# Expert MLP kernel: the last three tiles reordered, with seven up products between the halves of tile 14's main product and six more ahead of tile 15's

## What is computed

```
x = x + ffn0(cond0(x))      # cond0: mix of the 64 channels by a kernel made from cond; ffn0: 8 experts, top 2, 1024x1024 each
x = x + ffn1(cond1(x))      # cond1: grouped 1D convolution, 9 taps, plus a context term
                            # ffn1: main = c1 @ weight.T
                            #       gates = gw2(relu(layernorm(c1 @ gw1.T))), top 2, softmax, capacity over all tokens
                            #       lora = sum over experts of (c1 @ lora_A[e]) * w[e] @ lora_B[e] / 16
                            #       out = main + lora
```

## Time and profile before

| | us |
|---|---|
| median of 3 runs | 852.18 |
| lowest, highest | 850.26, 853.11 |
| the profiled execution | 853.87 |
| its span in the trace | 852.0 |
| TensorE busy in the span | 816.2 |
| VectorE busy in the span | 399.9 |

### The profile page before, as it was taken

The page is one execution under the profiler, slowest core; times in us unless marked ns, Lnnn a source line. Parts: engine busy times, 40 slices in busy tenths (PEclk is TensorE's granted clock), DMA queues, the critical chain, the costliest instruction groups (busy, mean ns, idle before and its releaser), DMA issues.

```text
span 852.0 us, 13067 instructions
## 1 busy us (share of the span) xinstructions
PE 816.2 (96%) x4260; PEld 674.0 (79%) x4261; DVE 399.9 (47%) x920; ACT 216.5 (25%) x335; POOL 90.4 (11%) x137
## 2 busy tenths in 40 slices
PE   6999599999999999999999999999999999999985
PEld 5555488888888888888888888888898898889863
DVE  1388650241514215142151151486566566656597
ACT  2344241342514325242252242300100010000100
POOL 1000121011110111011110012121112111100000
PEclk9999699999999999999999999999999999999998
DMA  8888479373555525555255254675545644520048
GB/s 284 347 323 311 176 278 418 114 256 127 185 183 181 201 86 184 184 169 213 86 174 192 90 197 132 214 204 140 126 98 139 147 108 107 155 58 25 1 137 258
DMA packets 61652, 149.26 MB, mean 175 GB/s; under 512 B 6928, under 2 KB 23584, under 8 KB 60704
## 3 DMA queue, kind: packets, MB, share of 16 engines
q1 hardware_dynamic: 40960, 93.41, 33.4%
q0 software_dynamic: 9968, 36.19, 14.6%
q10 hardware_dynamic: 10704, 19.41, 6.0%
HBM read 100.74 MB, written 39.85 MB: 165 GB/s over the span
## 4 chain that ended last, share of the span: by engine, by line
PE 81%; DMA 6%; DVE 6%; issue 3%; ACT 2%; SPq 1%; ACTq 1%; DVEq 0%; POOL 0%; POOLq 0%
PE bank L1283 58%; PE bank L1322 6%; PE bank L1181 4%; PE bank L1331 4%; PE bank L1274 3%; DMA work<-in_expert_w 3%; PE bank L1385 1%; DVE work L1116 1%; PE bank L1158 1%; DVE weights L937 1%; PE bank L1229 1%; PE bank L1204 1%; PE bank L1144 1%; DMA work<-y_scratch,pos_c 1%; DMA x1p<-res 1%
## 5 line engine op out<-in xcount | busy, mean ns | idle before, releaser
L1283 PE MATMUL bank<-weights,l_hi 128*128 128x512 f32 x1696 | 523.8, 390 | 0.0
L1283 PEld LDWEIGHTS bank<-weights,l_hi 128*128 128x128 f32 x1696 | 319.4, 188 | 64.6
L1283 PE MATMUL bank<-weights,l_lo 128*128 128x512 f32 x848 | 336.0, 396 | 2.5 <-DVE l_lo L905 2.4
L1283 PEld LDWEIGHTS bank<-weights,l_lo 128*128 128x128 f32 x848 | 159.7, 188 | 35.5 <-issue 4.5
L905 DVE TENSOR_TENSOR l_lo<-bank,l_hi 128x512 fp32r<-128x512 f32 x37 | 25.6, 692 | 184.0 <-ACT l_hi L684 184.0
L937 DVE TENSOR_TENSOR weights<-work,weights 128x1024 fp32r<-128x1024 f32 x64 | 76.2, 1223 | 55.1 <-ACT weights L695 54.8
L695 ACT ACTIVATE weights<-work 128x1024 fp32r<-128x1024 f32 x64 | 65.1, 1054 | 45.9 <-DMA work<-in_expert_w 27.6
L540 POOL DMA_INDIRECT work<-c_scratch,idx x37 | 42.4, 1146 | 196.2 <-PE bank L1274 195.9
L1322 PE MATMUL bank<-conv_sb,x1p 128*128 128x128 f32 x512 | 59.8, 275 | 1.1 <-DMA x1p<-res 1.1
L1322 PEld LDWEIGHTS bank<-conv_sb,x1p 128*128 128x128 f32 x512 | 58.8, 192 | 1.4 <-DMA x1p<-res 1.3
L735 ACT ACTIVATE l_hi<-work 128x512 fp32r<-128x512 f32 x32 | 18.4, 621 | 158.4 <-PE bank L1283 157.8
(11 more groups left out here) (174 smaller groups left out, 514.5 us busy)
## 6 DMA issues: line engine op xcount, KB each, us to landing
work<-in_expert_w SPq DMA_DIRECT2D x68, 512.0 KB, 6.3
y_scratch<-work ACTq DMA_DIRECT2D x74, 256.0 KB, 2.0
res<-in_x SPq DMA_DIRECT2D x16, 512.0 KB, 14.4
c_scratch<-work SPq DMA_DIRECT2D x16, 512.0 KB, 3.0
out<-work SPq DMA_DIRECT2D x16, 512.0 KB, 4.2
res<-in_x_ph SPq DMA_DIRECT2D x14, 512.0 KB, 5.4
x1p<-res SPq DMA_DIRECT2D x112, 64.0 KB, 4.6
work<-in_x_t SPq DMA_DIRECT2D x6, 1024.0 KB, 6.9
```

The source lines that it names most:

```text
L1283: mm = pe.matmul(to[:, :], a[:, k, :], b[:, k, cols * HALF:(cols + 1) * HALF], start=(k == 0 and n == 0), stop=(k == HC - 1 and n == 2))
```

## The change

The weights of layer 1 come in natural column order (the phase order is now made for the expert weights alone), so main's and up's results are natural, and `res` alone is in phase order. `take_main` does the turn of columns and writes its sum to `result(t)`, the rows of `res` of tile t-1 (a new tensor `first_out` for tile 0). The add after an up product, `take_up`, works in place on contiguous halves. The ring is gone: stores read `result(t)`. Up products use three pairs of banks, and wait for the adds of tile t-3.

The end of the tile loop is written out. Combines of tiles 14 and 15 both stand in step 12; conv(15) follows conv(14) into banks 6 and 7; down(14) and down(15) come before main(13). Tiles 13, 14, 15 have `c1` rows of their own, tile 14 also its own `l_hi2`, `l_lo2`. The rest is ordered as the new program of TensorE shows; tile 15's up product accumulates into main(15)'s banks (`more`), so there are 15 separate up products.

```diff
@@ program.sync
+            def store(t, cols):
+                to = out[tile_rows(t), cols].rearrange("(m c) n -> c m n", c=CP)
+                sp.dma_start(to, result(t)[:, cols]).then_inc(s_out, 16)
+
+            for t in range(EARLY_UPS):
+                sp.wait_ge(s_fin, 2 * (t + 1))
+                store(t, slice(0, H))
+            sp.wait_ge(s_me0, NT + CREDIT)
+            store(NT - 1, slice(0, HALF))
...
+            sp.wait_ge(s_me1, NT + CREDIT)
+            store(NT - 1, slice(HALF, H))
@@ program.scalar
+            round_c(NT - 2)
+            root(NT - 2)
+            root(NT - 1)
...
+                act.activation(up_hi[:, h, :], lora_sb[:, h * HALF:(h + 1) * HALF], ACT.Copy).then_inc(s_uh, 1)
             act.wait_ge(s_d2, 1)
             act.activation(we[:, :], wd[:, :], ACT.Exp).then_inc(s_ex2, 1)
...
+            round_c(NT - 1)
@@ program.vector
+            def take_main(t, halves=range(2)):
+
+                rows = res[:, bass.ds(t, 1), :].rearrange("p o (q w) -> p (o w) q", q=PH)
+                to = result(t).rearrange("p (w q) -> p w q", q=PH)
+                for h in halves:
+                    w = slice(h * P // 2, (h + 1) * P // 2)
+                    dve.wait_ge((s_m0, s_m1)[h], t + 1)
+                    dve.tensor_tensor(to[:, w, :], bank[h][:, :].rearrange("p (w q) -> p w q", q=PH), rows[:, w, :],
+                                      ALU.add).then_inc((s_me0, s_me1)[h], 1)
...
+            def take_up(t):
+                for h in range(2):
+                    half = result(t)[:, h * HALF:(h + 1) * HALF]
+                    dve.wait_ge(s_up, t * 2 + h + 1)
+                    dve.tensor_tensor(half, bank[2 + t % 3 * 2 + h][:, :], half, ALU.add).then_inc(s_fin, 1)
@@ program.tensor
+            down(NT - 3)
+            conv(0, NT // 2 * (PH * 16), (NT - 2) * 2)
+            conv(1, NT // 2 * (PH * 16), None, 6)
             down(NT - 2)
-            conv(1, NT // 2 * (PH * 16), (NT - 1) * 2)
-            main(NT - 2)
             down(NT - 1)
-            main(NT - 1, True)
-
-
+            main(NT - 3)
+            pe.wait_ge(s_a2, NT + CREDIT)
+            pe.matmul(bank[2][:, 0:2 * E], ones, acc2[:, :], start=True, stop=True).then_inc(s_t2, 1)
+            main(NT - 2, [0])
             for q in range(TQ):
...
             pe.wait_ge(s_ul, 2)
...
+            ups(range(FIRST_UPS))
+            main(NT - 2, [1])
+            ups(range(FIRST_UPS, EARLY_UPS))
+            main(NT - 1, [0], True)
+            ups(range(EARLY_UPS, NT - 1))
+            main(NT - 1, [1], True)
```

More of the change, by code:

```diff
@@ L41 @@
 QP = P // QUAD
+SPARE = 640
+FIRST_UPS = 7
+EARLY_UPS = 13
 LOADED = [2, 3, 4, 5, 6, 7]
@@ L175, in build @@
         warm = sb("warm", [P, 2])
+        with nc.sbuf_tensor("first_out", [P, H], F32) as first_out:
+            pass
         h0 = sb("h0", [P, B])
@@ L1098, in _ @@
                                   ALU.subtract).then_inc(s_ul, 1)
-            take_main(NT - 1)
+            rest_c(NT - 1)
+            dve.wait_ge(s_me1, NT - 2 + CREDIT)
+            take_main(NT - 2, [0])
             for q in range(TQ):
@@ L1104, in _ @@
                                   ALU.subtract).then_inc(s_tl, 1)
[L1106 to L1117, removed]
+            def take_up(t):
+                for h in range(2):
+                    half = result(t)[:, h * HALF:(h + 1) * HALF]
+                    dve.wait_ge(s_up, t * 2 + h + 1)
+                    dve.tensor_tensor(half, bank[2 + t % 3 * 2 + h][:, :], half, ALU.add).then_inc(s_fin, 1)
+            for t in range(FIRST_UPS):
+                take_up(t)
+            take_main(NT - 2, [1])
+            for t in range(FIRST_UPS, EARLY_UPS):
+                take_up(t)
+            take_main(NT - 1, [0])
+            for t in range(EARLY_UPS, NT - 1):
+                take_up(t)
+            take_main(NT - 1, [1])
         @program.tensor
@@ L1310, in _, with conv @@
             pe.wait_ge(s_late, 64)
-            def conv(j, landed, free):
+            def conv(j, landed, free, to=4):
                 pe.wait_ge(s_rel[j], landed)
@@ L1330, in down, with up, main @@
                 for k in range(HC):
-                    mm = pe.matmul(bank[2][:, 0:G1W], c1[:, k, :], down_sb[:, k, :], start=(k == 0), stop=(k == HC - 1))
+                    mm = pe.matmul(bank[2][:, 0:G1W], c1_of(t)[:, k, :], down_sb[:, k, :], start=(k == 0), stop=(k == HC - 1))
                 mm.then_inc(s_g1, 1)
[L1334 to L1340, removed]
+            def up(t, to, h, start):
+                q, at = t // TG, (t % TG) * P
+                for n, (a, b) in enumerate(((twt_lo, up_hi), (twt_hi, up_hi), (twt_hi, up_lo))):
+                    mm = pe.matmul(to[:, :], a[:, q, at:at + P], b[:, h, :], start=(start and n == 0), stop=(n == 2))
+                return mm
+            def main(t, halves=range(2), more=False):
+                for h in halves:
+                    pe.wait_ge((s_me0, s_me1)[h], t + CREDIT)
                     for k in range(HC):
```

163 lines of the change are left out of this document (95 added, 68 removed).

## The result

| | before | after |
|---|---|---|
| median, us | 852.64 | 842.87 |
| lowest and highest of 4 runs | 850.26, 853.82 | 842.50, 845.93 |
| the profiled execution | 853.87 | 845.93 |
| its span | 852.0 | 844.2 |

The ratio of the times is 0.9897, with a 95% interval of 0.9865 to 0.9929: 1.0% faster. The span fell by 7.8 us, where 7.6 was forecast. The medians are 9.8 apart, because the profiled execution of after lies 3.1 us above its median, as the longest of its four runs, and that of before only 1.2. A later set of runs of the same kernel gave 845.38 and, against its own runs of before, a ratio of 0.9905 (0.9876 to 0.9934).

What follows compares the result with a forecast made beforehand. TensorE was taken to bound nearly everywhere, VectorE the tail at 1.94 us a tile. Walking TensorE's new order ended at 844.4 against 852.0, 7.6 less; 852.18 - 7.6 gave 844.6 us, range 842.4 to 848.4.

Steps and rivals of the forecast that it cites:

- What bounds the end: Last stage before the change: VectorE sets the pace with two adds of 0.97 us, 1.94 us a tile; TensorE needs 1.36.
- Loop steps: Tile loop: turned adds in take_main cost VectorE 0.37 us more each, covered by 3.4 us; nothing lost, period stays 16.64.
- Rival C: Tile loop: turned adds delay TensorE in 14 steps, so the kernel is slower; one us beyond cover gives 858.6; chance 0.03.
- Downs: Behind conv(15): new waits of 0.4 us ahead of down(14) and 0.8 ahead of down(15), 1.2 us in all.
- The gap: Ahead of the first up product: TensorE idles 1.9 us from 799.3 until VectorE's twt_lo; before, this gap was 0.21.
- Up products: Tail: six matmuls take 1.36 us a product, VectorE's adds 1.20 a tile; waits bounded at 0.12 a product, 1.8 us.
- The end: Behind TensorE's last matmul: last add ends at 840.8, store issued at 841.0, lands in 3.0 us, plus 0.44: 844.4.
- The step from span to median: Whole kernel: the span difference of 7.6 us was subtracted from before's median of 852.18, giving 844.6.
- Rival A: Behind the new gap ahead of the up products: TensorE's clock falls to half, costing 3 us, 847.6; chance 0.07.
- Rivals B: Reordered tail: VectorE or SP is later at downs, gap or tile 15's spread, costing 1 to 3 us, 847; chance 0.12.
- D: Up products: plain in-place adds cost 0.97 us like turned ones, so some 5 us remain, 849.6; chance 0.04.
- Stores: End: 16 stores took 28.3 us of full DMA, 1.8 us each, and drain while the tail spreads them over 37 us.

Runs made afterwards that it cites:

- e_plain: Before's order and two pairs of banks kept, only columns turned in main's add, plain adds behind up products, stores reading the rows; 845.17 us, ratio 0.9913 to before.
- e_turned_up: The changed kernel with adds behind the up products reading a turned constant operand, values not the reference's; 845.59 us, ratio 0.9926 to before.
- e_twt_first: The changed kernel with VectorE's twt_lo right behind up_lo, rest_c(15) and half of take_main(14) behind the first seven adds; 842.75 us, ratio 0.990 to before.
- e_12_13: The changed kernel with twelve up products ahead of main(14)'s second half and one behind it, in place of seven and six; 844.17 us, ratio 0.9904 to before.
- after_again: The changed kernel run again without edit; 845.38 us, ratio 0.9905 to before.
- after_third: The changed kernel run once more without edit; 842.81 us in one run.
- e_store_whole: The changed kernel with tile 15 stored by one 512 KB DMA behind its last add, in place of two halves; 844.42 us in one run.
- e_0_0: The changed kernel with all 15 up products between main(15)'s halves, none ahead of main(14)'s second half; 841.32 us, ratio 0.9874 to before.
- e_long_gap: The changed kernel with two dummy VectorE subtractions ahead of twt_lo, lengthening the gap before the first up product; 846.81 us, ratio 0.9931 to before.
- e_no_gaps: The changed kernel with main's halves reordered to cover TensorE's three tail waits, eight up products before main(15)'s first half; 841.21 us, ratio 0.9875 to before.

## Why the prediction was right, and where it was not

The forecast was 844.6 in a range of 842.4 to 848.4, the measured median 842.87.

*What bounds the end.* Right. VectorE set 0.97 us an add; e_plain and e_turned_up each took that bound away in their own way, and each was some 6 us shorter.

*Loop steps.* Right: the period is 16.64 in both kernels. VectorE paid 11.4 us more in the loop stage, all covered. Rival C is out.

*Downs.* down(14) was to start 0.4 us late and down(15) 0.8; the chain has them at 775.49 and 778.50, and main(13) at 780.91, where the sum had 780.95 plus a start. The two runs without waits are shorter by 2.7 and 3.0 us, close to the 3.0 that both waits and the gap come to.

*The gap.* Forecast 1.9 us, measured 1.84; e_twt_first gives 1.7 of it back by the length, though not by the median time.

*Up products.* Mis-sized a little. I took main's 0.227 us a matmul; 42, 36 and 15 of them took 9.87, 8.26 and 3.45, that is 0.229 to 0.235. All of it makes 0.5 us. The bound of 0.12 us a product for waits was not needed: VectorE was never late.

*The end.* The last add ends at 840.88, forecast 840.8. The last store landed in 2.9 us, forecast 3.0. The span was 844.2, forecast 844.4: 3.3 us lie behind the last add, where the sum had 3.6, and this error and that of the up products are against each other. The prediction's other estimate for this landing, 2.6 us, was 0.3 too low; the section that it is worked out from describes DMAs that GpSimd issues, and SyncE issues this one.

*The step from span to median.* This is the part that was off by 1.7 us, inside the range. I subtracted the difference of two spans from a median of three. The starts of down(12) in the thirteen profiles run from 746.13 to 749.44, and before and after happened to be the two latest. That cancels in the difference of spans, but not in the median of four of after, of which three lie at 842.5 to 842.9. The range had to hold this spread. That the two profiles start down(12) within 0.05 us of each other, so that the spans differ by what the tail gives, was luck.

*Rival A, the clock.* I gave it 0.07, on the ground that the gap is shorter than the 3.43 us of the earlier trace rows. That ground was wrong, and so was the other one: not 30 us of unbroken matmuls stand ahead of the gap but some 20, for the sum itself has a wait ahead of down(15). Six profiles have a gap of 1.84 us (after, e_turned_up, e_12_13, after_again, after_third, e_store_whole), and in two of them the clock fell. The price was 1.7 us, not 3. By these profiles the chance should have been near a third, and the price half of a slowed stretch of 3.4 us. It did not decide the result: 1.7 us is within the range. A granted clock under 1.00 behind 799 us was one of the forecast's own signs of being wrong; that the profile of after doesn't show it, and two of its kind do, was luck.

*Rivals B and D.* Not seen. For D, e_turned_up shows that even adds at 0.98 us would have cost 1.8 us and not the 5 that I gave it: VectorE catches up under main's halves, where it waits again for 1.30 us. What the third pair of banks adds to this was not tested apart. The chances of faster by more add up to 0.95 by their own terms, not 0.94.

*Stores.* The 1.8 us a store was wrong, as told above; it did not enter the sum, but it made me expect a loss in e_0_0 that isn't there.

What stays open in part: why the stretch ahead of the tail differs by 3.3 us between executions. The first gather starts at 91.75 to 95.66 us in these profiles, and the rank order of the starts of down(12) only partly follows it. Two pieces are TensorE's clock. Around 90 to 107 us it is at 0.50 for 17.1 us in after, e_plain, e_twt_first, e_long_gap and e_no_gaps, and for 13.7 in the other eight. And the earlier trace rows are not its only fall: in before, e_0_0 and e_turned_up it fell near 38 us as well, for 3.4 us. Stages of before there:

```profile
34.00:38.00 4.00, 2.79 (x29) 1.86 (x28) 1.25 (x8) 2.70 (x4) 0.00 (x0) 1.00 0.59 238
38.00:41.50 3.50, 3.50 (x8) 1.58 (x6) 2.19 (x11) 0.34 (x1) 0.00 (x0) 0.51 0.99 337
```

and the second of them in after, where TensorE had been busy for the same 2.79 of 4.00 us:

```profile
38.00:41.50 3.50, 3.50 (x13) 1.83 (x13) 3.33 (x22) 1.27 (x2) 0.00 (x0) 1.00 1.01 335
```

The longest wait of TensorE ahead of that fall is 0.8 us. So one long gap is not needed; a stretch with several short waits had it too, again in some executions only. In before's end stage, on the other hand, 14 waits of up to 0.6 us, 4.4 in all, left the clock at 1.00.

## What to carry to other kernels

When one engine sets the pace of a last stage, both a cheaper operation and other work between give most of the same gain, so price them together and not as a sum. Then look at the order of what is left on the engine that was the bound: here 2.2 us of VectorE work that nobody waited for stood ahead of what TensorE waited for, and moving it gave 1.7 us by the length, which the median times can't confirm. Compare variants over a stretch that starts behind the noise, such as a step of a steady loop, when they differ by less than single executions do.

## What was not expected of the hardware

TensorE's clock fell to 1.2 GHz behind a gap of 1.84 us in two of six profiles, 1.3 to 1.4 us after work had come back, for 3.4 us, and cost 1.7 us. In the one profile with a gap of 3.05 us it fell inside the gap and cost 2.7 us. In three of thirteen profiles it fell near 38 us, behind waits of at most 0.8 us. Stores of 512 KB that followed each other without a pause went at 361 to 371 GB/s, against the 240 GB/s of before's end, which VectorE had fed.
